# GpSimd makes three of the sixteen u*B products of a state-space scan

## The chip, the cores and the metric

The kernel runs on one core of one Trainium2 chip. The metric is the device time of one launch in microseconds. Before the change it is 1684.95 us, the median of three runs (1680.35 to 1686.84).

## The reference

A decoder block in float32 on x of shape (4, 1024, 256): a state-space block (Mamba), cross attention over 154 context positions with 16 heads, and a mixture of four experts with the best two weighted, each with a residual and a layer norm. The change touches the first.

```python
x_ssm, z = split(x @ W_in.T)                 # 512 channels each
x_ssm = silu(causal_conv(x_ssm, 4 taps) + conv_b)
proj = x_ssm @ W_x.T                         # B (16), C (16), dt (1) per token
dt = softplus(proj[..., -1:] * W_dt + b_dt)
A = -exp(A_log)                              # (512, 16)
def step(h, inp):                            # over 1024 tokens
    dA = exp(dt_t[..., None] * A)
    h = dA * h + (x_t * dt_t)[..., None] * B_t[:, None, :]
    y = einsum('bdn,bn->bd', h, C_t)
y = (y + x_ssm * D) * silu(z)
x = layernorm(x + y @ W_out.T)
```

## The kernel before

The tokens are worked in 16 chunks of 256 (four per batch). Channels lie on the partitions: 512 channels are four tiles, so u, dt, a decay or a state of one state index n is 128 x 4 x 256. A chunk runs through n = 0 to 15, each in two halves h of two channel tiles (128x512).

For each n, TensorE spreads B's row over the partitions in PSUM (`b_row`, L368); VectorE multiplies it with u into one of three PSUM banks (`make_bu`, L945), adds the carried state to the first column where the chunk isn't a batch's first (`add_carry`, L961) and scans: state = decay * previous + u*B (`scans`, L970). ScalarE makes the decays, exp(dt*A), four instructions for an n (`step`, L686), and copies the last column of a state out (L684). GpSimd multiplies the state by C (L900), and TensorE transposes and adds these into y (`add_state`, L384). Decay, state and state*C each have a ring of four buffers. In the first column of each tile the decay is zero, so that the two tiles of a half don't mix.

While chunk i is scanned, chunk k = i + 1 is prepared and chunks i - 1 and i - 2 are finished. Nothing schedules this at run time: each engine has a list of (place, work), and work with place n stands behind its instructions for state n of chunk i. On TensorE, at each place, `b_row(n + 2)` and `add_state(n - 2)` stand ahead of the work. The places that matter here:

- TensorE: input projection 0 and 1, convolution halves 2 and 4 (`conv`, L305), z tiles 5 and 6 (L316), `project` 8.
- ScalarE: `take_xi` 3 and 4, `take_conv` 5 and 7 (L595), `take_z` 8 and 9 (L600), silus 10, `copies` 11 (L616, L617), `terms` and `softplus` 12 (L632 to L642), `next_lead` 13 (L626), `take_y_back` 14 and 15. The norm of chunk i - 2: `spreads` 3, `guess` 6, `normalise` 9 (L667).
- GpSimd: `split` 8 and 10 (L844, L848), `make_dt` 10 (L814, waits for the softplus), `first_arg` 10, `make_u` 11 (L819), `injections` 12 and 4 (L836); the norm: `centre` 0 (L863), `variance` 2, `newton` 4 (L868 to L878), on tiles of two columns.
- VectorE: `take_y` of chunk i - 1 (L933) inside state 2.

SyncE stores each chunk's C rows to DRAM and loads them back spread over all partitions (`load_c`). In the first chunk it also loads all weights of the attention and the experts. The second block (`attn_ffn_block`) starts when the first has ended.

## Time and profile before

| what | value |
|---|---|
| median of three runs | 1684.95 us |
| the profiled execution | 1675.18 us, span 1673.4 us |
| VectorE busy | 1465.3 us (88%) |
| TensorE busy (matmuls) | 1335.8 us (80%) |
| ScalarE busy | 1114.0 us (67%) |
| GpSimd busy | 915.1 us (55%) |
| mean granted TensorE clock | 0.919 |
| state-space block | about 0 to 999 us |

Busy time is the time in which at least one instruction runs on the engine. Successive instructions of VectorE, ScalarE and GpSimd overlap by some hundredths of a microsecond, so what one costs in a full queue is read from start to start. In the trace "step_area" is dt and u (and later the rows of maxima), "c_area" the spread C rows, "weights" the convolution's input and weights, "y_sb" also the z tile.

### The profile page before, as it was taken

To read this page: it belongs to the slowest core of one execution; us is meant where nothing else is said; L and a number is where in the kernel's file an instruction comes from. 1 tells how busy PE (TensorE), PEld (TensorE's weight loads), DVE (VectorE), ACT (ScalarE), POOL (GpSimd) and SP (SyncE) were. 2 spreads that over 40 slices of the span, in tenths; PEclk is the share of its full clock that TensorE was granted. 3 is DMA by queue.
4 is the path that set the end of the run, shared out by engine and by line. 5 is a ranking of instruction groups with operands and counts; after the bars stand their busy time and mean duration, and the time that the engine had idled before them with its cause. 6 is when DMAs were issued, how large, how long until landed. Compare 5 with 4: busy or idle time off the path is not lost. (4 is left out here: it accounts for less than half of the span.)

```text
span 1673.4 us, 22601 instructions
## 1 busy us (share of the span) xinstructions
PE 1335.8 (80%) x7484; PEld 930.7 (56%) x7484; DVE 1465.3 (88%) x2698; ACT 1114.0 (67%) x2452; POOL 915.1 (55%) x663
## 2 busy tenths in 40 slices
PE   7687778788777877787886969988988898887880
PEld 5566556666656666565665644446445644462460
DVE  5999999999999999999999966697869786978578
ACT  5867887788788778878877524337633763375570
POOL 1778878877887788788778701102710271027015
PEclk9889899989989898998898989999999999999895
DMA  7201210220122022102102012100010000000000
GB/s 234 67 14 45 70 58 13 70 70 32 40 70 71 1 70 70 50 21 70 64 1 89 14 38 103 36 1 1 26 55 1 1 26 26 1 1 1 25 1 25
DMA packets 37927, 69.87 MB, mean 42 GB/s; under 512 B 3569, under 2 KB 31570, under 8 KB 33586
## 3 DMA queue, kind: packets, MB, share of 16 engines
q1 hardware_dynamic: 37810, 68.43, 12.0%
q8 instruction: 59, 0.97, 0.2%
q14 instruction: 58, 0.48, 0.1%
HBM read 59.77 MB, written 8.65 MB: 41 GB/s over the span
## 5 line engine op out<-in xcount | busy, mean ns | idle before, releaser
L900 POOL TENSOR_TENSOR state_c<-state,c_area 128x1024 f32<-128x1024 f32 x256 | 602.0, 2362 | 167.8 <-DVE state L970 148.9
L970 DVE TENSOR_TENSOR_SCAN state<-decay,ps 128x512 f32<-128x512 f32 x512 | 620.6, 1212 | 0.0
L686 ACT ACTIVATE decay<-step_area,negA 128x255 f32<-128x255 f32 x1024 | 432.6, 496 | 0.4 <-DVE step_area L1049 0.4
L945 DVE TENSOR_TENSOR ps<-step_area,ps 128x512 f32<-128x512 f32 x512 | 349.7, 683 | 8.0 <-PE ps L368 6.2
L384 PE MATMUL ps<-ident_sb,state_c 128*128 128x128 f32 x2048 | 293.3, 291 | 12.9 <-POOL state_c L900 11.9
L1578 POOL TENSOR_TENSOR big<-big,g_sb 128x1024 f32<-128x1024 f32 x29 | 79.4, 2739 | 406.6 <-ACT big L1467 404.9
L384 PEld LDWEIGHTS ps<-ident_sb,state_c 128*128 128x128 f32 x2048 | 253.5, 151 | 39.0 <-POOL state_c L900 21.5
L368 PE MATMUL ps<-parts,sel_bc_sb 96*128 96x256 bf16 x256 | 74.7, 292 | 102.7 <-DVE ps L961 80.2
L1391 PE MATMUL ps<-w_sb,weights 128*128 128x512 f32 x256 | 122.6, 615 | 0.0
L1426 PE MATMUL ps<-w_sb,hT 128*128 128x256 f32 x512 | 120.0, 388 | 2.4 <-ACT hT L1536 1.9
L1666 DVE BATCH_NORM_STATS2 stats<-big 128x6 f32<-128x256 f32 x256 | 88.4, 413 | 30.4 <-ACT big L1541 21.1
L368 PEld LDWEIGHTS ps<-parts,sel_bc_sb 96*128 96x128 bf16 x256 | 25.8, 101 | 151.3 <-DVE ps L961 113.5
L305 PE MATMUL ps<-weights 128*128 128x256 f32 x480 | 108.5, 378 | 0.0
L1426 PEld LDWEIGHTS ps<-w_sb,hT 128*128 128x128 f32 x512 | 96.8, 194 | 18.7 <-ACT hT L1536 5.1
L1646 DVE TENSOR_REDUCE step_area<-ps 128x8 f32<-128x1232 f32 x48 | 69.0, 1437 | 34.0 <-PE ps L1287 33.9
L1521 ACT ACTIVATE big<-ps 128x1024 f32<-128x1024 f32 x32 | 32.8, 1024 | 98.3 <-PE ps L1391 98.3
L305 PEld LDWEIGHTS ps<-weights 128*128 128x128 f32 x480 | 88.5, 189 | 11.2
L1582 POOL TENSOR_TENSOR acc<-acc,big 128x256 f32<-128x256 f32 x116 | 86.3, 744 | 9.1
L288 PE MATMUL ps<-weights 128*128 128x256 f32 x240 | 64.0, 414 | 29.7 <-ACT weights L586 29.7
L356 PE MATMUL ps<-w_out_sb,y_sb 128*128 128x256 f32 x256 | 77.2, 456 | 0.0
L1478 ACT ACTIVATE hT<-ps 128x1024 f32<-128x1024 f32 x64 | 62.0, 1020 | 20.1 <-PE ps L1319 20.1
L1391 PEld LDWEIGHTS ps<-w_sb,weights 128*128 128x128 f32 x256 | 45.8, 192 | 49.6 <-issue 47.3
(211 smaller groups left out, 2357.9 us busy)
## 6 DMA issues: line engine op xcount, KB each, us to landing
c_area<-c_scratch SPq DMA_DIRECT2D x32, 1024.0 KB, 6.5
weights<-in_xT SPq DMA_DIRECT2D x16, 256.0 KB, 3.1
...
weights<-x_scratch SPq DMA_DIRECT2D x4, 1024.0 KB, 8.1
xa<-x_scratch SPq DMA_DIRECT2D x4, 1024.0 KB, 5.6
out_x<-acc SPq DMA_DIRECT2D x4, 1024.0 KB, 4.4
w_sb<-in_w SPq DMA_DIRECT2D x2, 1024.0 KB, 13.0
```

Source lines behind the costliest of these rows:

```text
L305: last = nc.tensor.matmul(w_ps[:, e * TC + skip:(e + 1) * TC], diag_w[:, TAPS - 1 - back, j, :], xi[:, j, HALO + skip - back:HALO + TC - b ...
L368: nc.tensor.matmul(b_ps[n % 2][:, 0:TC], sel_bc_sb[:, n, :], parts[:, i[1] % 2, :], start=True, stop=True)\
L384: last = nc.tensor.matmul(y_ps[:, t * DI + j * P:t * DI + (j + 1) * P], state_c[:, n % RING, j, t * P:(t + 1) * P], ident_sb[:, :], start= ...
L686: nc.scalar.activation(decay[:, n % RING, j, 1:], dt_sb[:, i[1] % 2, j, 1:], ACT.Exp, scale=negA[:, j * NS + n:j * NS + n + 1]).then_inc(s ...
L900: nc.gpsimd.tensor_tensor(state_c[:, n % RING, :, :], state[:, n % RING, :, :], c_bc[:, q, n, :].unsqueeze(1).to_broadcast([P, CT, TC]), A ...
L945: nc.vector.tensor_tensor(bu_ps[m % 3][:, :].rearrange("p (j n) -> p j n", j=2), u_sb[:, i[1] % 2, 2 * h:2 * h + 2, :], b_ps[n % 2][:, 0:T ...
L970: nc.vector.tensor_tensor_scan(state[:, n % RING, pair, :].rearrange("p j n -> p (j n)"), decay[:, n % RING, pair, :].rearrange("p j n -> ...
L1391: last = nc.tensor.matmul(dst, xT[:, k, t * P:(t + 1) * P], w1_sb[:, k, h * HALF:(h + 1) * HALF], start=False, stop=k == KT - 1, skip_grou ...
L1426: last = nc.tensor.matmul(dst, hT[:, e * KT + k, i * P:(i + 1) * P], w2_sb[:, e * KT + k, :], start=False, stop=k == KT - 1, skip_group_ch ...
L1578: nc.gpsimd.tensor_tensor(tile, tile, g2_sb[:, :], ALU.mult).then_inc(s_gm, 1)
L1582: nc.gpsimd.tensor_tensor(acc[:, t, :], acc[:, t, :], tile[:, e * DM:(e + 1) * DM], ALU.add).then_inc(s_sum, 1)
L1666: nc.vector.bn_stats(stats[:, i * E + e, :], big[:, n, i, e * DM:(e + 1) * DM]).then_inc(s_st, 1)
```

## The change

For n = 2, 5 and 8 (`OFF`) GpSimd multiplies u by B's row into a new SBUF tile `ub` (two buffers) and adds the carried state there. The B rows for this come through DRAM like the C rows, into `b_bc`. The PSUM bank that had held u*B of these n now takes their decay: ScalarE writes zeros into its first columns and the exponentials into the rest, one step later than the decays of the other n, and waits for the bank (`psum_decay`). The scan of these n reads decay from PSUM and u*B from SBUF. TensorE leaves out their B rows.

GpSimd's norm uses operations with two constants in place of pairs, and its places and ScalarE's change. The loads of w1 and w2 move to the start of the second block, since their space is taken.

```diff
+        OFF, APART = (2, 5, 8), 3
+        KEPT = [n for n in range(NS) if n not in OFF]
...
             def load_c(k):
-                sp.dma_start(c_dram[bass.ds(at(k, NS), NS), :], proj[NS:BC, q, :]).then_inc(s_cst, 16)
+                sp.dma_start(bc_dram[bass.ds(at(k, BC), BC), :], proj[0:BC, q, :]).then_inc(s_cst, 16)
...
+                if not is_first(k):
+                    sp.wait_ge(s_ub, at(k, 2 * NO))
+                rows = bc_dram[bass.ds(at(k, BC, OFF[0]), APART * NO), :].rearrange("(a s) n -> a s n", s=APART)
+                sp.dma_start(b_bc[:, :, :], rows[:, 0, :].partition_broadcast(P)).then_inc(s_bb, 16)
...
             def step(i, n):
...
+                if n in KEPT:
+                    for j in range(CT):
+                        nc.scalar.activation(decay_tile(i, n)[:, j, 1:], dt_sb[:, i[1] % 2, j, 1:], ACT.Exp,
+                                             scale=negA[:, j * NS + n:j * NS + n + 1]).then_inc(s_decay, 1)
+                if n - 1 in OFF:
+                    psum_decay(i, n - 1)
+
+            def psum_decay(i, n):
+                for h in range(2):
+                    act.wait_ge(s_scan, bu_free(i, n, h))
+                    bank = bu_bank(i, n, h)[:, :].rearrange("p (j n) -> p j n", j=2)
+                    nc.scalar.activation(bank[:, :, 0], zeros[:, :], ACT.Copy)
+                    for e in range(2):
+                        j = 2 * h + e
+                        nc.scalar.activation(bank[:, e, 1:], dt_sb[:, i[1] % 2, j, 1:], ACT.Exp,
+                                             scale=negA[:, j * NS + n:j * NS + n + 1]).then_inc(s_decay, 1)
...
-                    work += [... (3, lambda: spreads(old)), (6, lambda: guess(old)),
-                             (9, lambda: normalise(old))]
+                    work += [... (5, lambda: spreads(old)), (8, lambda: guess(old)),
+                             (13, lambda: normalise(old))]
...
+            def product_b(i, n):
+                c, later = OFF.index(n), i[1] % CPB
...
+                nc.gpsimd.tensor_tensor(tile, u_sb[:, i[1] % 2, :, :], b_bc[:, c, :].unsqueeze(1).to_broadcast([P, CT, TC]),
+                                        ALU.mult).then_inc(s_ub, 1 if later else 2)
+                if later:
...
+                    pool.wait_ge(s_ub, at(i, 2 * NO, 2 * c + 1))
+                    nc.gpsimd.tensor_tensor(tile[:, :, 0], tile[:, :, 0], inject[:, n, :], ALU.add).then_inc(s_ub, 1)
...
-                    work += [(0, lambda: centre(old)), (2, lambda: variance(old)), (4, lambda: newton(old))]
+                    work += [(0, lambda: centre(old)), (3, lambda: variance(old)), (6, lambda: newton(old))]
...
+                work += [(1, lambda: product_b(i, OFF[1])), (4, lambda: product_b(i, OFF[2]))]
+                if prepare:
+                    work.append((14, lambda: product_b(k, OFF[0])))
...
             def scans(i, n, h):
...
+                if n in OFF:
...
+                    a, b = bu_bank(i, n, h)[:, :], flat(ub_tile(i, n))
+                else:
...
+                    a, b = flat(decay_tile(i, n)), bu_bank(i, n, h)[:, :]
...
-        LOADS = 4
+        LOADS = 6
+            sp.dma_start(w1_sb[:, :, :], w1).then_inc(s_const, 16)
+            sp.dma_start(w2_sb[:, :, :], w2).then_inc(s_const, 16)
```

GpSimd before, from `make_dt` (step_area<-step_area,relu) to the norm's variance of the next chunk; step_area<-step_area,xs is `make_u`:

```order
L814 TENSOR_TENSOR step_area<-step_area,relu 128x1024 [waits s_sp]
L826 TENSOR_TENSOR first_dA<-step_area,negA 128x64 [waits s_dt]
L848 TENSOR_TENSOR parts<-rest,lead 96x256 [waits s_lead]
L900 TENSOR_TENSOR state_c<-state,c_area 128x1024 [waits s_sum,s_scan]
L819 TENSOR_TENSOR step_area<-step_area,xs 128x1024 [waits s_dt]
L900 TENSOR_TENSOR state_c<-state,c_area 128x1024 [waits s_sum,s_scan]
L836 TENSOR_TENSOR inject<-first_dA,carry 128x48 [waits s_carry,s_dA]
L900 TENSOR_TENSOR state_c<-state,c_area 128x1024 [waits s_sum,s_scan] x3
L900 TENSOR_TENSOR state_c<-state,c_area 128x1024 [waits s_sum,s_scan,s_cb10]
L863 TENSOR_TENSOR mean<-total,coef 128x2 [waits s_r,s_norm]
L900 TENSOR_TENSOR state_c<-state,c_area 128x1024 [waits s_sum,s_scan] x2
```

The same place now, from the injections on:

```order
L891 TENSOR_TENSOR inject<-first_dA,carry 128x48 [waits s_carry,s_dA]
L972 TENSOR_TENSOR state_c<-state,c_area 128x1024 [waits s_sum,s_scan] x2
L941 TENSOR_TENSOR ub<-step_area,b_bc 128x1024 [waits s_scan,s_bb,s_u]
L947 TENSOR_TENSOR ub<-ub,inject 128x4 [waits s_ub,s_inj]
L972 TENSOR_TENSOR state_c<-state,c_area 128x1024 [waits s_sum,s_scan]
L972 TENSOR_TENSOR state_c<-state,c_area 128x1024 [waits s_sum,s_scan,s_cb10]
L915 TENSOR_SCALAR mean<-total 128x2 [waits s_r,s_norm]
L972 TENSOR_TENSOR state_c<-state,c_area 128x1024 [waits s_sum,s_scan]
L941 TENSOR_TENSOR ub<-step_area,b_bc 128x1024 [waits s_scan]
L947 TENSOR_TENSOR ub<-ub,inject 128x4 [waits s_ub]
L972 TENSOR_TENSOR state_c<-state,c_area 128x1024 [waits s_sum,s_scan] x2
```

One product with its small add stands between state*C 14 and 15, and one between state*C 1 and 2.

ScalarE before, from the second convolution half (xs<-ps,par_sb) to the silus, places 7 to 10; y_sb<-ps is a z tile:

```order
L595 ACTIVATE xs<-ps,par_sb 128x256 [waits s_in]
L595 ACTIVATE xs<-ps,par_sb 128x256
L684 ACTIVATE carry<-state 128x4 [waits s_scan]
L686 ACTIVATE decay<-step_area,negA 128x255 x4
L600 ACTIVATE y_sb<-ps 128x512 [waits s_in]
L684 ACTIVATE carry<-state 128x4 [waits s_scan]
L686 ACTIVATE decay<-step_area,negA 128x255 x4
L667 ACTIVATE res<-res,shift_sb,rstd 128x256 [waits s_nw]
L667 ACTIVATE res<-res,shift_sb,rstd 128x256
L600 ACTIVATE y_sb<-ps 128x512 [waits s_in]
```

The same place now:

```order
L637 ACTIVATE xs<-ps,par_sb 128x256 [waits s_in]
L637 ACTIVATE xs<-ps,par_sb 128x256
L724 ACTIVATE carry<-state 128x4 [waits s_scan]
L715 ACTIVATE lnv<-var 128x2 [waits s_nw]
L717 ACTIVATE rstd<-lnv 128x2 [waits s_ln]
L642 ACTIVATE y_sb<-ps 128x512 [waits s_in]
L724 ACTIVATE carry<-state 128x4 [waits s_scan]
L728 ACTIVATE decay<-step_area,negA 128x255 x4
L738 ACTIVATE ps<-zeros 128x2 [waits s_scan]
L741 ACTIVATE ps<-step_area,negA 128x255 x2
L738 ACTIVATE ps<-zeros 128x2 [waits s_scan]
L741 ACTIVATE ps<-step_area,negA 128x255 x2
```

Between the convolution and z tile 0 there is no decay any more; behind z tile 0 stand decay 9 and then decay 8, in PSUM. The normalisation has left this place.

VectorE now, from the carry add of state 0's second half to state 3 (order prints a scan as SCALAR_TENSOR_TENSOR; yg is `take_y`):

```order
L1033 TENSOR_TENSOR ps<-ps,inject 128x2 [waits s_bu]
L1017 TENSOR_TENSOR ps<-step_area,ps 128x512 [waits s_scan]
L1049 SCALAR_TENSOR_TENSOR state<-decay,ps 128x512 [waits s_decay,s_bu,s_sc]
L1033 TENSOR_TENSOR ps<-ps,inject 128x2 [waits s_bu]
L1049 SCALAR_TENSOR_TENSOR state<-decay,ps 128x512 [waits s_decay,s_bu]
L1049 SCALAR_TENSOR_TENSOR state<-ps,ub 128x512 [waits s_decay,s_ub,s_sc]
L1003 TENSOR_TENSOR yg<-ps,gate 128x1024 [waits s_gate,s_yb,s_sum]
L1017 TENSOR_TENSOR ps<-step_area,ps 128x512 [waits s_scan,s_b]
L1049 SCALAR_TENSOR_TENSOR state<-ps,ub 128x512 [waits s_decay]
```

Before, a product and a carry add stood ahead of each scan; now two products with their carry adds are missing here.

## Rows read from the trace of the kernel before

**Rows 1.** Windows: busy us of each engine (instructions), granted clock, DMA share, GB/s.
```profile
300.00:360.00 60.00, 46.89 (x264) 36.73 (x262) 59.76 (x92) 48.61 (x125) 46.97 (x33) 0.91 0.17 58
```

**Rows 2.** The page's part 5, the costliest groups of the block.
```profile
L900 POOL TENSOR_TENSOR state_c<-state,c_area 128x1024 f32<-128x1024 f32 x256 | 602.0, 2362 | 167.8 <-DVE state L970 148.9
L970 DVE TENSOR_TENSOR_SCAN state<-decay,ps 128x512 f32<-128x512 f32 x512 | 620.6, 1212 | 0.0
...
L945 DVE TENSOR_TENSOR ps<-step_area,ps 128x512 f32<-128x512 f32 x512 | 349.7, 683 | 8.0 <-PE ps L368 6.2
```

**Rows 3.** Timeline (start us, duration us, instruction), VectorE's `take_y`, four chunks apart.
```profile
268.51 1.20 DVE L933 TENSOR_TENSOR yg<-ps,gate 128x1024 f32<-128x1024 f32 x1
...
500.58 1.20 DVE L933 TENSOR_TENSOR yg<-ps,gate 128x1024 f32<-128x1024 f32 x1
```

**Rows 4.** Timeline of VectorE, half a state.
```profile
401.33 0.15 DVE L961 TENSOR_TENSOR ps<-ps,inject 128x2 f32<-128x2 f32 x1
401.38 0.68 DVE L945 TENSOR_TENSOR ps<-step_area,ps 128x512 f32<-128x512 f32 x1
401.98 1.21 DVE L970 TENSOR_TENSOR_SCAN state<-decay,ps 128x512 f32<-128x512 f32 x1
403.11 0.15 DVE L961 TENSOR_TENSOR ps<-ps,inject 128x2 f32<-128x2 f32 x1
```

**Rows 5.** Timeline of GpSimd, from `make_dt` to the next chunk's `centre`.
```profile
420.30 2.36 POOL L814 TENSOR_TENSOR step_area<-step_area,relu 128x1024 f32<-128x1024 f32 x1 [2.18 <-ACT step_area L642]
...
423.10 0.67 POOL L848 TENSOR_TENSOR parts<-rest,lead 96x256 bf16<-96x256 f32 x1
...
430.90 9.33 POOL L900 TENSOR_TENSOR state_c<-state,c_area 128x1024 f32<-128x1024 f32 x4
440.19 0.19 POOL L863 TENSOR_TENSOR mean<-total,coef 128x2 f32<-128x2 f32 x1
```

**Rows 6.** Timeline of TensorE, `add_state(2)` and the second convolution half.
```profile
392.78 1.04 PE L384 MATMUL ps<-ident_sb,state_c 128*128 128x128 f32 x8
393.66 3.62 PE L305 MATMUL ps<-weights 128*128 128x256 f32 x16
```

**Rows 7.** Timeline of ScalarE, from the second convolution half to `next_lead`.
```profile
397.32 0.84 ACT L595 ACTIVATE xs<-ps,par_sb 128x256 f32<-128x256 f32 x2 [2.39 <-PE ps L305]
...
398.14 1.70 ACT L686 ACTIVATE decay<-step_area,negA 128x255 f32<-128x255 f32 x4
400.23 0.60 ACT L600 ACTIVATE y_sb<-ps 128x512 f32<-128x512 f32 x1 [0.39 <-PE ps L316]
...
402.42 1.08 ACT L667 ACTIVATE res<-res,shift_sb,rstd 128x256 f32<-128x256 f32 x2
...
421.82 0.49 ACT L626 ACTIVATE lead<-rest,par_sb 96x256 bf16<-96x256 f32 x1
```

**Rows 8.** Timeline of GpSimd, two dependent small operations of the norm.
```profile
396.99 0.20 POOL L870 TENSOR_TENSOR newt<-newt,var 128x2 f32<-128x2 f32 x1
397.26 0.20 POOL L872 TENSOR_TENSOR newt<-newt,coef 128x2 f32<-128x2 f32 x1
```

**Rows 9.** Line 1578, later block: durations ns min/median/max, first and last start us.
```profile
L1578 POOL TENSOR_TENSOR big<-big,g_sb x29: 2354/2366/4667, 1158.7 to 1649.0; 128x1024 f32<-128x1024 f32 x29
```

**Rows 10.** Line 814, `make_dt`, in the same form.
```profile
L814 POOL TENSOR_TENSOR step_area<-step_area,relu x15: 2349/2358/2365, 72.7 to 884.5; 128x1024 f32<-128x1024 f32 x15
```

**Rows 11.** The page's part 6, loads of w1 and w2.
```profile
w_sb<-in_w SPq DMA_DIRECT2D x2, 1024.0 KB, 13.0
```

**Rows 12.** The last constant's issue; VectorE's first wait behind the constants (line 1775).
```profile
1002.01 0.43 SPq L1201 DMA_DIRECT2D before_sb<-in_before  x1
...
L1775 DVEq EVENT_SEMAPHORE  x4: 21/21/50, 1035.8 to 1533.4; - x4
```

**Rows 13.** Timeline of TensorE behind an idle time of 2.39 us.
```profile
406.87 0.40 PE L368 MATMUL ps<-parts,sel_bc_sb 96*128 96x256 bf16 x1 [2.39 <-DVE ps L961]
407.05 1.92 PE L384 MATMUL ps<-ident_sb,state_c 128*128 128x128 f32 x8
```

More of the change, by code:

```diff
@@ L43, with mamba_block @@
 TG = 4
-def mamba_block(nc, x, xT, w_in, w_x, w_out, par, ident_sb, ident, sel_bc, sel_p, c_dram, x1, ahead, s_ahead, ps, early, late, shared,
+def mamba_block(nc, x, xT, w_in, w_x, w_out, par, ident_sb, ident, sel_bc, sel_p, bc_dram, x1, ahead, s_ahead, ps, early, late, shared,
                 w, ctxT):
@@ L64, in mamba_block @@
         SKIP_AT = 8
+        OFF, APART = (2, 5, 8), 3
+        KEPT = [n for n in range(NS) if n not in OFF]
+        NO, NK = len(OFF), len(KEPT)
+        USERS = [(n, h) for n in range(NS) for h in range(2)]
+        EMIT = []
+        for n in range(NS):
+            if n in KEPT:
+                EMIT.append(n)
+            if n - 1 in OFF:
+                EMIT.append(n - 1)
         w_ssm, diag_w, xi, w_gate, xT_sb, w_x_sb = (early[n] for n in ("w_ssm", "diag_w", "xi", "w_gate", "xT", "w_x"))
@@ L83, in mamba_block @@
         state_c = sb("state_c", [P, RING, CT, TC])
+        ub = sb("ub", [P, 2, CT, TC])
+        b_bc = sb("b_bc", [P, NO, TC])
+        zeros = sb("zeros", [P, 2])
         carry = sb("carry", [P, NS, CT])
@@ L130, in mamba_block @@
         s_par = sem("s_par")
-        s_coef = sem("s_coef")
         s_in = sem("s_in")
@@ L148, in mamba_block @@
         s_bu = sem("s_bu")
+        s_ub = sem("s_ub")
+        s_bb = sem("s_bb")
         s_scan = sem("s_scan")
@@ L186, in shift, with rank, scanned, bu_bank @@
             return (i[0], i[1] + n)
+        def rank(n):
+            return sum(m < n for m in KEPT)
+        def scanned(i, n, h):
+            return at(i, 2 * NS, 2 * RING + 2 * n + h + 1)
+        def bu_bank(i, n, h):
+            return bu_ps[at(i, len(USERS), USERS.index((n, h))) % 3]
+        def bu_free(i, n, h):
+            p = USERS.index((n, h))
+            return scanned(i if p >= 3 else shift(i, -1), *USERS[p - 3])
+        def decay_tile(i, n):
+            return decay[:, at(i, NK, rank(n)) % RING, :, :]
+        def ub_tile(i, n):
+            return ub[:, at(i, NO, OFF.index(n)) % 2, :, :]
         def is_first(i):
@@ L364, in b_row @@
             def b_row(i, n):
+                if n in OFF:
+                    return
                 if n == 0:
                     pe.wait_ge(s_split, at(i, 2, 2))
-                pe.wait_ge(s_bu, at(i, 4 * NS, 4 * n + 4))
+                before = n - 4 if n - 2 in OFF else n - 2
+                if before >= 0:
+                    pe.wait_ge(s_bu, at(i, 4 * NK, 8 + 4 * rank(before) + 4))
+                else:
+                    pe.wait_ge(s_bu, at(i, 4 * NK, 4 * n + 4))
                 nc.tensor.matmul(b_ps[n % 2][:, 0:TC], sel_bc_sb[:, n, :], parts[:, i[1] % 2, :], start=True, stop=True)\
@@ L905, in turn @@
                             what()
+            nc.gpsimd.memset(zeros[:, :], 0.0)
             nc.gpsimd.memset(decay[:, :, :, 0], 0.0).then_inc(s_zero, 1)
-            for c, value in enumerate((0.5, 1.5, 1.0 / DM, LN_EPS, -1.0 / DM)):
-                nc.gpsimd.memset(coef[:, c, :], value).then_inc(s_coef, 1)
-            half, one_half, per_dm, eps, minus_per_dm = (coef[:, c, :] for c in range(5))
             pool.sem_inc(s_sum, RING)
@@ L917, in _ @@
             injections(first, 0, NS - RING)
+            product_b(first, OFF[0])
             turns(pool, turn)
@@ L1063, in _, with attn_ffn_block @@
             round_neg(1)
-def attn_ffn_block(nc, x1, ctxT, ident_sb, w, ps, late, shared, bo, g2, be2, bias_rows, before, out):
+def attn_ffn_block(nc, x1, ctxT, ident_sb, w, w1, w2, ps, late, shared, bo, g2, be2, bias_rows, before, out):
     U = G * NL
@@ L1931, in decoder_block @@
             ahead.append((w[name][tuple(slice(None) for _ in shape)], source))
-        mamba_block(nc, x, xT, w_in, w_x, w_out, par, ident_sb, ident, sel_bc, sel_p, c_dram, x1, ahead, s_ahead, ps, early, late,
+        mamba_block(nc, x, xT, w_in, w_x, w_out, par, ident_sb, ident, sel_bc, sel_p, bc_dram, x1, ahead, s_ahead, ps, early, late,
                     shared, w, ctxT)
-        attn_ffn_block(nc, x1, ctxT, ident_sb, w, ps, late, shared, bo, g2, be2, bias_rows, before, out)
+        attn_ffn_block(nc, x1, ctxT, ident_sb, w, channels(w1), channels(w2), ps, late, shared, bo, g2, be2, bias_rows, before, out)
 def _constants():
```

96 lines of the change are left out of this document (52 added, 44 removed).

## Prediction

> **What bounds the kernel now.** I read the page first. Part 1 has VectorE busy for 88% of the span; the slices of part 2 show that in the first 58% (the state-space block) it is full, while ScalarE and GpSimd are at seven or eight tenths. A 60 us window in the middle has VectorE at 59.76 of 60, ScalarE at 48.61 and GpSimd at 46.97 [rows 1]. The costly groups are the scans, the u*B products and GpSimd's state*C [rows 2]. So each chunk lasts as long as VectorE needs. Two of VectorE's `take_y`, four chunks apart, are at 268.51 and 500.58 [rows 3]: 58.0 us a chunk.
>
> Durations on VectorE overlap, so I take start to start from its timeline [rows 4]: carry add 0.05, product 0.60, scan 1.13, together 1.78 for half a state, 3.55 for a state. 16 x 3.55 plus 1.1 for `take_y` is 57.9; a batch's first chunk has no carry adds.
>
> Then I looked for the second longest thing: a ring of waits through three engines that closes once a chunk. I call D the start of GpSimd's `make_dt` (L814). From D GpSimd runs without a gap to its `centre`, 420.30 to 440.19, 19.9 us [rows 5]; this covers the make_dt and make_u of the next chunk and the state*C of states 11 to 15 and 0. Then come state*C 1 and 2. TensorE's `add_state(2)` needs state*C 2, and the second convolution half stands behind it in TensorE's order: 0.88 from add to convolution [rows 6], 3.66 to ScalarE's `take_conv(k, 1)` at 397.32 [rows 6, 7]. From there ScalarE works to the softplus, which releases the next D: 23.0 us, 397.32 to 420.30 [rows 5, 7]. The sum is 19.9 + 0.2 (centre) + 2.33 + 2.36 (state*C, a quarter of the 9.33 of four, and a last one in full) + 0.05 + 0.88 + 3.66 + 23.0 = 52.4 us. It is under 57.9, so today this ring has 5.5 us of slack and VectorE rules.
>
> **VectorE.** For states 2, 5 and 8 two products and two carry adds go: 6 x (0.60 + 0.05) = 3.9 us a chunk, 3.6 in a batch's first chunk. Against it, `add_carry(n-1, 1)` now stands directly ahead of its scan, without a product between: 0.1 us each, three times (the carry add is 0.15 long and 0.05 of that is hidden now [rows 4]). The scans keep their shape and one operand in PSUM, so 1.13 stays. Net 3.6 a chunk: VectorE alone would need 54.3.
>
> **GpSimd.** A product is a 128x1024 two-input operation, as state*C with 2.36 [rows 2, 5]. The carry add behind it waits for it: a waiting small operation starts 0.07 after the one before and takes 0.20 [rows 8]. So 2.6 us, three times a chunk: 7.8. The norm loses two small operations, 2 x 0.27 [rows 8]. GpSimd's busy 46.97 of 60 is 45.4 of 58.0; it becomes some 52.7. By itself that is still under 54.3. But two of the three products (state 2 at place 14, state 5 at place 1) lie inside the ring's GpSimd part: +5.2. What waits behind the one at place 1 is state*C 2, and for that TensorE with its convolution. The product of state 8 (place 4) lies outside the ring.
>
> The rule that could make this product dearer is the Trainium skill's "GPSIMD Engine Reference", section 1: GpSimd's SBUF interface is shared with VectorE, with contention when VectorE has two SBUF inputs. The same form on GpSimd in the later block has a median of 2366 ns and a maximum of 4667 [rows 9], which that could be. The new scan reads decay from PSUM and u*B from SBUF, one SBUF input as before, so by that rule too 2.36 holds; with 4.67 for each product the ring would be 4.6 us longer.
>
> **ScalarE.** The decays of 2, 5 and 8 are written one step later, behind those of 3, 6 and 9, and each half waits for its PSUM bank. What counts is the ring's part. Before, decay 8 (1.70, at 398.14) lay in the time in which ScalarE waited for TensorE's z tile at 400.23 [rows 7]: it cost nothing. Now only `guess` stands there, and decay 8 follows decay 9, behind z tile 0, on the path: +1.6, and two writes of zeros, for which no row stands: between the 0.05 of a hidden small operation [rows 4] and the 0.27 of a waiting one [rows 8] I take 0.1 each: +1.8. The norm's `normalise` (1.08, of which 0.1 overlaps) leaves the stretch: -0.98. It now stands ahead of `next_lead`, which was at 421.82 with 0.49 [rows 7], so the lead is ready at 423.3 where GpSimd's `parts` started at 423.10 [rows 5]: +0.25. The exponentials that write PSUM have no row. Bounds: the SBUF form is 0.42 each (1.70 for four), the one that reads PSUM is 0.42 (0.84 for two) [rows 7]; I take 0.40 start to start, bounds 0.2 and 0.6, which moves the ring by 0.8 us either way. The Trainium skill ("ScalarE: Activation LUTs", Profile) says that PSUM is the lower-latency destination for ScalarE; no row here shows it, and it would speak for the lower half.
>
> **The ring afterwards.** 52.4 + 5.2 + 1.8 - 0.98 + 0.25 = 58.6 us (57.9 where the chunk is a batch's first: an injection and two small adds are missing, each 0.2 to 0.27 as in [rows 8]). That is more than VectorE's 54.3 and a little more than today's 58.0. So VectorE gets a wait of about 4 us a chunk, and the chunk is not shorter.
>
> Other ways round are shorter. Via convolution half 0, decay 6, the late decay 5, and the rest of ScalarE to the softplus: 22.7 (GpSimd to the end of state*C 0) + 5.2 + 0.8 + 1.8 + 1.9 + 1.8 + 23.8 = 58.0, close behind. Via VectorE's scan 7, which frees the bank of decay 8's second half: about 57.
>
> **The sum.** L814 runs from 72.7 (chunk 1) to 884.5 (chunk 15) [rows 10]: 14 turns in 811.8 us. Now 3 x 57.9 + 11 x 58.6 = 818.3: +6.5. The first D comes about 1 us later (decay 8's 1.8 less some 0.8 that VectorE is ahead by then). The last chunk prepares no next one, so the ring is open there and VectorE's gain counts: up to -3.9; ScalarE's transposes of the attention stand in that chunk, so -3 (bounds -3.9 and 0). Together +4.5.
>
> The rest is hidden. w1 and w2 (1 MB each; two such took 13.0 us to land [rows 11]) are issued after 1002.01, and the first wait of VectorE behind the constants passes at 1035.8 [rows 12]: 33 us of cover; without it, up to 10 us. Their absence at the start frees queue time that nobody waited for. The small store of B and C and the load of three rows of B are asked for at ScalarE's copies and needed at place 14, over 10 us later. The shorter norm in the tail stands beside VectorE's row of maxima: 0.
>
> On the profiled execution's time: 1675.2 + 4.5 = 1679.7. That execution is 9.8 below the median of 1684.95; against the median, which is what I forecast for, 1684.95 + 4.5 = 1689.
>
> **Rivals.** B: VectorE stays the bound, because the ring has an overlap that I count in series. Full busy share in [rows 1] speaks for it, the sum above against. Then 12 x 3.6 + 4 x 3.4 = 57 us less: 1628.
>
> C, the slower side: TensorE's clock. Today TensorE's b_row waits for VectorE in small pieces; in the new order it waits for state*C 2 after an early convolution half 0, some 1.4 to 2 us idle, just ahead of the second half. After 2.39 us idle at 406.87, eight transposes took 1.92, against 1.04 at 392.78 [rows 6, 13]: the 1.2 GHz level against 2.4. At that level add_state is 0.9 longer and the convolution's 3.46 doubles. It decides if TensorE idles there as long as it did at 406.87. If the clock falls in every chunk, that is +4.3 x 14 = 60 us: 1749; in half of them, 1719. For it: the ring leaves TensorE longer idle. Against: in the rows the slow stretch followed on other sparse time, and the convolution stands behind a busy stretch.
>
> E: the ring is shorter than I sum it, mostly by cheaper PSUM writes and small overlaps, near 57.5 a chunk: -15 in 14 turns, and -3 in the last: 1668.
>
> **How the numbers follow.** The measurement can tell about 0.5% (8.4 us) from no change. Forecast 0.50; of it 0.42 within 0.5% (bounds of the PSUM writes and the last chunk: -5 to +8), 0.08 slower, where the rings next to it interfere. B 0.15, faster. C 0.27, slower. E 0.08, faster. So faster 0.23, same 0.42, slower 0.35. Range: from 1660, which takes in E but not B, to 1730, which takes in C in two chunks of three; left out are B and the last third of C, about 0.2.
>
> **What would show it.** Right: L814 about 58.5 apart, VectorE at some 93% of a chunk, its waits on ScalarE's or GpSimd's result, GpSimd without a gap from make_dt to state*C 2, ScalarE's decay 8 behind z tile 0. Wrong: VectorE still at 99% with D 54 to 55 apart (B); convolution groups of 6 us with the granted clock at 0.5 (C); products on GpSimd well over 2.4 us.

## The result, and the profile after

The changed kernel takes 1692.74 us (median; 1689.78 to 1695.24, without one execution of 2077.16 us in which the granted clock was 0.61), beside 1681.24 us of the kernel before on the same chip (1676.16 to 1686.84, seven runs). The ratio is 1.0065, 95% interval 1.0042 to 1.0088: slower, by little. 1689 was forecast, from a median of before that was 1684.95 then. The forecast difference was +4.5 us; the medians differ by 11.5. The two profiled executions differ by 17.6 (1692.74 and 1675.18), because the profiled execution of before is 6 us under its median.

The first look is at GpSimd's `make_dt`, now L869, in the form of [rows 10] (durations in ns, first and last start in us):

```profile
L869 POOL TENSOR_TENSOR step_area<-step_area,relu x15: 2347/2350/2363, 76.8 to 897.1; 128x1024 f32<-128x1024 f32 x15
```

Fourteen turns take 897.1 - 76.8 = 820.3 us, 58.6 each; before they took 58.0. The same window as in [rows 1], then a long one of both kernels, after first (busy us of TensorE's matmuls, its weight loads, VectorE, ScalarE and GpSimd, with instructions; granted clock, DMA share, GB/s):

```profile
300.00:360.00 60.00, 45.43 (x257) 36.48 (x256) 54.82 (x76) 48.95 (x132) 52.77 (x36) 0.90 0.15 56
100.00:900.00 800.00, 616.12 (x3426) 498.26 (x3423) 743.79 (x1084) 649.41 (x1721) 714.54 (x471) 0.90 0.16 57
```

```profile
100.00:900.00 800.00, 629.91 (x3507) 504.82 (x3505) 794.97 (x1243) 649.66 (x1668) 629.92 (x430) 0.91 0.15 52
```

VectorE, which was busy for 99% of the block, now idles 56 of 800 us, 4.1 a chunk. Its busy time fell from 57.6 to 54.5 us a chunk, and all of it came back as idle time. What it waits for, of the kernel after, grouped by line between 100 and 900 us (busy us and mean ns, then idle us ahead of the group and who ended it; L1049 are scans, L1017 u*B products, L1003 `take_y`):

```profile
L1049 DVE TENSOR_TENSOR_SCAN state<-decay,ps 128x512 f32<-128x512 f32 x355 | 429.1, 1211 | 3.3 <-ACT decay L728 2.0
L1017 DVE TENSOR_TENSOR ps<-step_area,ps 128x512 f32<-128x512 f32 x356 | 243.2, 683 | 33.6 <-issue 17.4 <-PE ps L410 16.1
L1049 DVE TENSOR_TENSOR_SCAN state<-ps,ub 128x512 f32<-128x512 f32 x83 | 100.6, 1213 | 6.9 <-ACT ps L741 6.1
L1003 DVE TENSOR_TENSOR yg<-ps,gate 128x1024 f32<-128x1024 f32 x13 | 15.9, 1224 | 12.4 <-issue 12.4
```

One turn in detail. GpSimd from one `make_dt` to state*C 2, to compare with [rows 5] (start, duration, instruction, idle time before it in brackets; ub is the new product):

```profile
427.50 2.35 POOL L869 TENSOR_TENSOR step_area<-step_area,relu 128x1024 f32<-128x1024 f32 x1 [2.25 <-ACT step_area L684]
...
430.57 0.67 POOL L903 TENSOR_TENSOR parts<-rest,lead 96x256 bf16<-96x256 f32 x1 [0.23 <-ACT lead L668]
...
443.02 2.37 POOL L941 TENSOR_TENSOR ub<-step_area,b_bc 128x1024 f32<-128x1024 f32 x1
445.54 0.20 POOL L947 TENSOR_TENSOR ub<-ub,inject 128x4 f32<-128x4 f32 x1
445.69 4.66 POOL L972 TENSOR_TENSOR state_c<-state,c_area 128x1024 f32<-128x1024 f32 x2
...
452.81 2.36 POOL L941 TENSOR_TENSOR ub<-step_area,b_bc 128x1024 f32<-128x1024 f32 x1
455.25 0.20 POOL L947 TENSOR_TENSOR ub<-ub,inject 128x4 f32<-128x4 f32 x1
455.39 2.36 POOL L972 TENSOR_TENSOR state_c<-state,c_area 128x1024 f32<-128x1024 f32 x1
```

TensorE behind it, as [rows 6]:

```profile
458.35 0.28 PE L410 MATMUL ps<-parts,sel_bc_sb 96*128 96x256 bf16 x1 [0.47 <-DVE ps L1033]
458.47 1.04 PE L426 MATMUL ps<-ident_sb,state_c 128*128 128x128 f32 x8
459.35 3.60 PE L341 MATMUL ps<-weights 128*128 128x256 f32 x16
```

ScalarE behind that, as [rows 7], from `take_conv(k, 1)` to the second z tile:

```profile
462.99 0.84 ACT L637 ACTIVATE xs<-ps,par_sb 128x256 f32<-128x256 f32 x2
...
465.90 0.60 ACT L642 ACTIVATE y_sb<-ps 128x512 f32<-128x512 f32 x1 [1.65 <-PE ps L352]
466.39 0.20 ACT L724 ACTIVATE carry<-state 128x4 f32<-128x4 f32 x1
466.49 1.69 ACT L728 ACTIVATE decay<-step_area,negA 128x255 f32<-128x255 f32 x4
468.08 0.15 ACT L738 ACTIVATE ps<-zeros 128x2 f32<-128x2 f32 x1
468.18 0.86 ACT L741 ACTIVATE ps<-step_area,negA 128x255 f32<-128x255 f32 x2
468.97 0.15 ACT L738 ACTIVATE ps<-zeros 128x2 f32<-128x2 f32 x1
469.07 0.86 ACT L741 ACTIVATE ps<-step_area,negA 128x255 f32<-128x255 f32 x2
469.86 0.58 ACT L642 ACTIVATE y_sb<-ps 128x512 f32<-128x512 f32 x1
```

This is the predicted ring: GpSimd has no gap but the 0.23 on the lead, state*C 2 ends 30.2 us after D, the convolution follows, and decay 8 stands behind z tile 0, 1.78 us from its first zero to the next z tile. The next D comes at 486.77, 23.8 us after `take_conv`. One row differs: `b_row(6)`, ahead of `add_state(2)` in TensorE's order, waited for VectorE until 458.35, some 0.6 after GpSimd's result was there. A branch through VectorE runs beside the ring and was last in this turn. ScalarE came to `take_conv` without idle time, where [rows 7] have 2.39: the decays ahead of it, the late one of 5 among them, had just ended.

This turn is one of three of 59.2 to 59.3 us. The three in which a batch's first chunk is scanned took 57.8 to 57.9, the other eight 58.4 to 58.75. What the three long ones have in common is the second half of TensorE's input projection: 2.93, 3.32 and 2.88 us, where the other eleven took 1.89. The granted clock was 0.64, 0.55 and 0.65 in these stretches and 1.00 at 390.26. The projection of the turn shown, then that of the turn before it (D at 368.75), with what follows there on TensorE and, last, ScalarE's `take_conv(k, 1)`:

```profile
449.65 2.93 PE L324 MATMUL ps<-weights 128*128 128x256 f32 x8
```

```profile
390.26 1.89 PE L324 MATMUL ps<-weights 128*128 128x256 f32 x8
...
398.92 0.28 PE L410 MATMUL ps<-parts,sel_bc_sb 96*128 96x256 bf16 x1 [1.45 <-DVE ps L1033]
399.06 1.09 PE L426 MATMUL ps<-ident_sb,state_c 128*128 128x128 f32 x8
399.99 3.62 PE L341 MATMUL ps<-weights 128*128 128x256 f32 x16
...
403.65 0.84 ACT L637 ACTIVATE xs<-ps,par_sb 128x256 f32<-128x256 f32 x2 [1.02 <-PE ps L341]
```

In this ordinary turn state*C 2 ends at 399.0, 30.3 after D, `take_conv` comes 4.6 later and the next D 23.85 after that: 58.75. `b_row(6)` was only 0.1 ahead of `add_state(2)`, so the branch through VectorE is about as long here too.

Where the 17.6 us of the two profiled executions are:

| stretch | before | after | difference |
|---|---|---|---|
| start to the first D | 72.7 | 76.8 | +4.1 |
| 14 turns | 811.8 | 820.3 | +8.5 |
| last D to the last scan | 72.6 | 76.4 | +3.8 |
| rest | 716.3 | 717.5 | +1.2 |

### The profile page after: what moved, and what is told of

Read it like the earlier page. It is cut to its first block and busy times, and to the rows that moved or that the text cites. A ratio compares the mean times of both kernels' runs of the same rounds, so it can differ in the third digit from the quotient of the medians.

```text
span 1691.0 us, 22427 instructions
## 1 busy us (share of the span) xinstructions
PE 1333.7 (79%) x7436; PEld 934.6 (55%) x7436; DVE 1412.8 (84%) x2530; ACT 1123.9 (66%) x2548; POOL 1023.6 (61%) x711
## 5 line engine op out<-in xcount | busy, mean ns | idle before, releaser
L1049 DVE TENSOR_TENSOR_SCAN state<-decay,ps 128x512 f32<-128x512 f32 x416 | 502.6, 1211 | 4.3 <-ACT decay L728 2.8
L728 ACT ACTIVATE decay<-step_area,negA 128x255 f32<-128x255 f32 x832 | 351.4, 496 | 0.5 <-DVE step_area L1127 0.5
L426 PE MATMUL ps<-ident_sb,state_c 128*128 128x128 f32 x2048 | 296.2, 293 | 53.5 <-POOL state_c L972 53.2
L1017 DVE TENSOR_TENSOR ps<-step_area,ps 128x512 f32<-128x512 f32 x416 | 284.0, 683 | 45.3 <-PE ps L410 26.1
L426 PEld LDWEIGHTS ps<-ident_sb,state_c 128*128 128x128 f32 x2048 | 256.2, 152 | 97.3 <-POOL state_c L972 72.7
L941 POOL TENSOR_TENSOR ub<-step_area,b_bc 128x1024 f32<-128x1024 f32 x48 | 113.4, 2362 | 28.7 <-DVE step_area L1130 28.7
L1049 DVE TENSOR_TENSOR_SCAN state<-ps,ub 128x512 f32<-128x512 f32 x96 | 116.4, 1212 | 10.5 <-ACT ps L741 9.2
L341 PE MATMUL ps<-weights 128*128 128x256 f32 x480 | 108.5, 378 | 0.0
L383 PE MATMUL ps<-ident_sb,yg 128*128 128x128 f32 x128 | 26.9, 347 | 82.6 <-ACT y_sb L688 70.2
L361 PE MATMUL ps<-xs,weights 128*97 128x256 f32 x120 | 49.6, 585 | 44.3 <-ACT xs L648 44.3
L410 PE MATMUL ps<-parts,sel_bc_sb 96*128 96x256 bf16 x208 | 61.9, 298 | 27.4 <-DVE ps L1033 20.9
L741 ACT ACTIVATE ps<-step_area,negA 128x255 f32<-128x255 f32 x192 | 82.3, 460 | 0.0
```

Source lines behind the costliest of these rows:

```text
L341: last = nc.tensor.matmul(w_ps[:, e * TC + skip:(e + 1) * TC], diag_w[:, TAPS - 1 - back, j, :], xi[:, j, HALO + skip - back:HALO + TC - b ...
L426: last = nc.tensor.matmul(y_ps[:, t * DI + j * P:t * DI + (j + 1) * P], state_c[:, n % RING, j, t * P:(t + 1) * P], ident_sb[:, :], start= ...
L728: nc.scalar.activation(decay_tile(i, n)[:, j, 1:], dt_sb[:, i[1] % 2, j, 1:], ACT.Exp, scale=negA[:, j * NS + n:j * NS + n + 1]).then_inc( ...
L941: nc.gpsimd.tensor_tensor(tile, u_sb[:, i[1] % 2, :, :], b_bc[:, c, :].unsqueeze(1).to_broadcast([P, CT, TC]), ALU.mult).then_inc(s_ub, 1 ...
L1017: nc.vector.tensor_tensor(bu_bank(i, n, h)[:, :].rearrange("p (j n) -> p j n", j=2), u_sb[:, i[1] % 2, 2 * h:2 * h + 2, :], b_ps[n % 2][:, ...
L1049: nc.vector.tensor_tensor_scan(state[:, n % RING, pair, :].rearrange("p j n -> p (j n)"), a, b, 0.0, ALU.mult, ALU.add).then_inc(s_scan, 1)
```

## Experiments

All ratios are to the kernel before, run on the same chip in turns. "D to D" is the start of `make_dt` in the last chunk less that in the first, over 14, and VectorE's idle time is that between 100 and 900 us.

| kernel | ratio (95% interval) | D to D | VectorE idle |
|---|---|---|---|
| before | 1 | 58.0 | 5.0 |
| after | 1.0065 (1.0042 to 1.0088) | 58.6 | 56.2 |
| before, gate cut | 1.0008 (0.9980 to 1.0036) | 58.2 | 7.8 |
| after, gate cut | 1.0005 (0.9980 to 1.0030) | 57.95 | 49.3 |
| before, extra products | 1.0200 (1.0165 to 1.0236) | 60.2 | 2.3 |
| after, extra products | 1.0103 (1.0065 to 1.0141) | 58.6 | 26.2 |
| after, state 5's product at place 2 | 1.0044 (1.0017 to 1.0072) | 58.3 | 53.2 |
| before with the norm's part alone | 0.9980 (0.9949 to 1.0010) | 58.0 | 6.1 |
| states 8, 11, 14 | 1.0136 (1.0099 to 1.0173) | 59.6 | 71.8 |
| states 6, 9 | 1.0069 (1.0041 to 1.0096) | 58.5 | 45.7 |
| states 3, 6, 9 | 1.0030 (1.0008 to 1.0053) | 57.9 | 54.6 |
| states 2, 5 | 0.9968 (0.9943 to 0.9992) | 57.4 | 28.2 |
| states 2, 5; 5 at place 2 | 0.9964 (0.9947 to 0.9980) | 57.3 | 27.7 |
| state 2 | 0.9889 (0.9864 to 0.9914) | 57.1 | 11.0 |

### Who bounds each kernel

Two pairs test it from both sides. The first makes ScalarE's part of the ring shorter, in both kernels: the gate's silu, one instruction of 1.0 us, works on 16 of its 1024 columns from the third chunk on.

```diff
-                nc.scalar.activation(gate[:, q, :, :], zc[:, :, :], ACT.Silu).then_inc(s_gate, 1)
+                few = DI if k[1] < 2 else 8
+                nc.scalar.activation(gate[:, q, :, 0:few], zc[:, :, 0:few], ACT.Silu).then_inc(s_gate, 1)
```

> The kernel before, with ScalarE's silu of the gate cut to 16 of its 1024 columns from chunk 2 on (the output is then not the reference's). It stands in ScalarE's stretch between the second convolution half and the softplus and takes 1.04 us there. Ring theory (before, the ring ScalarE - GpSimd - TensorE has 5.5 us of slack and VectorE rules): no change, 1681, within 0.2%. Rival (ScalarE's work bounds the chunk in both kernels): 13 x 0.95 = 12 us less, 1669.

> The changed kernel with the same cut of the gate's silu (output not the reference's). Ring theory (the ring closes and bounds the chunk): make_dt to make_dt gets 0.95 shorter, 13 x 0.95 = 12 us less than the changed kernel's 1692.7, so 1680, about level with before. Rival 1 (VectorE still bounds, and what it gained is lost in waits for the late decays in PSUM): under 4 us. Rival 2 (GpSimd's 52.7 us of work bound it): 0.

The kernel before took 1681.39 us, no change. The one after took 1684.18, 8.5 under its 1692.74; its turn fell from 58.6 to 57.95. So a microsecond of ScalarE's time is worth nothing before and most of a microsecond a chunk after. That less than the whole came back (0.65 a turn) has two parts in the trace: the turns with a batch's first chunk hardly moved (57.85 to 57.8), and the ordinary ones fell by 0.8 (58.6 to 57.8). A second way round close behind would do that; which one was not settled.

The second pair makes VectorE's work longer: four products more in a chunk, into a spare tile.

```diff
+                if n in (10, 12):
+                    dve.wait_ge(s_extra, at(i, 4, (n - 10) + h))
+                    nc.vector.tensor_tensor(spare[:, :, :], ...).then_inc(s_extra, 1)
```

> The kernel before with VectorE making four more products of 128x512 per chunk (n = 10 and 12, into a spare tile that nobody reads): 4 x 0.6 = 2.4 us of VectorE per chunk. Ring theory (VectorE rules before): 16 x 2.4 = 38 us more, 1719. Rival (VectorE was not the bound before): under 10 us.

> The changed kernel with the same four extra products of VectorE per chunk. Ring theory: VectorE has some 4 us of waits in each chunk, so most of the 2.4 is hidden; 0 to 10 us more than 1692.7, so 1693 to 1703, and most of it in the last chunk (2.4) and where VectorE's delay meets TensorE's b_row. Rival 1 (VectorE bounds): 38 us more, 1731.

Before: 1710.96 us, 2.0% slower, and a turn of 60.2, +2.2 for 2.4 us of work. That is some 5 us less in all than expected. Some of it is idle time that VectorE still had and has no more (5.0 to 2.3 us in 800, 0.2 a turn); the rest stays unexplained. After: 1695.36 (ratio 1.0103 beside 1.0065, with intervals that overlap), and the turn is 58.6 as without them; VectorE's idle time fell from 56.2 to 26.2 us. `make_dt` of the kernel before with the extra products, then of after with them:

```profile
L816 POOL TENSOR_TENSOR step_area<-step_area,relu x15: 2347/2355/2365, 71.8 to 914.7; 128x1024 f32<-128x1024 f32 x15
```

```profile
L871 POOL TENSOR_TENSOR step_area<-step_area,relu x15: 2352/2358/2367, 75.7 to 896.1; 128x1024 f32<-128x1024 f32 x15
```

Before, VectorE is the bound; after, it has room for 2.4 us of work more. Both pairs together show the exchange of the bound, and exclude rival B.

### The parts of the change

The product of state 5 one place later, so that it stands behind state*C 2 and not ahead of it:

```diff
-                work += [(1, lambda: product_b(i, OFF[1])), (4, lambda: product_b(i, OFF[2]))]
+                work += [(2, lambda: product_b(i, OFF[1])), (4, lambda: product_b(i, OFF[2]))]
```

> The changed kernel with one number changed: GpSimd's product of state 5 at place 2 instead of 1, so behind state*C 2, on which TensorE's add_state(2) and the second convolution half wait. Ring theory, GpSimd branch (state*C 2 releases the second convolution half): 2.6 us leave the ring, but the next ring (VectorE's take_y and b_row(6), or the first half with decays 6 and 5) is only 0.6 shorter, so 0.3 to 0.8 us a chunk, 4 to 11 us less: 1682 to 1689. If the trace's branch through take_y and b_row(6) rules (there the second half started 0.6 us after add_state(2) could have): 0 to 3 us less. Rival (GpSimd's amount of work bounds): 0.

The time, 1690.07, is 2.7 us less, as the branch through VectorE would have it (0 to 3). A turn fell by 0.27 us on average, not by 2.6. The three turns with a batch's first chunk fell from 57.85 to 57.0; the ordinary ones stayed at 58.3 to 58.7. In those a way round that does not lead through state*C 2 is as long as the ring, and takes over at once. `b_row(6)` above is the likely one, and `take_y` another (it waited 1.04 us in the turn shown).

The norm's part alone, on the kernel before (fewer operations, their places, ScalarE's places):

> The kernel before with only the norm's part of the change: GpSimd's two operations fewer and the later places of the norm on GpSimd and ScalarE. Ring theory (VectorE rules before, the norm stands beside it): no change from before, within 0.2%. Rival (the norm's chain costs the chunk time): 2 to 5 us less.

1678.84 us, ratio 0.9980 with an interval that holds 1; first and last D at 72.7 and 884.5, as in [rows 10] to the digit. It does nothing where VectorE is the bound.

States 2 and 5 alone, state 8 as before (`OFF, APART = (2, 5), 3`, no product at place 4):

> The changed kernel with states 2 and 5 alone (state 8 as before: VectorE's product, decay in SBUF, made ahead of z tile 0). Ring theory: decay 8 leaves the path, 1.8 us less a chunk, 58.6 to 56.8; VectorE alone needs 57.9 - 2.4 = 55.5. So 14 x 1.8 = 25 us less than the changed kernel, with 2 to 5 lost again to rings beside it: 1668 to 1674, which is faster than before although VectorE keeps one product more. Rival (every product moved saves or costs the same): the change's +11 in proportion, 2/3 of it, 1689.

1675.95 us, ratio 0.9968, a turn of 57.4 instead of 58.6. That is short of the 1668 to 1674 that I expected: state 8 cost 1.2 us a chunk, of the 1.8 that its late decay is long on the path; its product lay outside. Two states moved is faster than three. Against before there is little in it: the last scan starts at 957.2 us in this trace and at 957.1 in that of before.

### Other choices of the states

If what stands in the ring decides, then states should be chosen by where their products and late decays fall. The first try had all three products outside GpSimd's part, at places 4, 6 and 9:

```diff
-        OFF, APART = (2, 5, 8), 3
+        OFF, APART = (8, 11, 14), 3
...
-                work += [(1, lambda: product_b(i, OFF[1])), (4, lambda: product_b(i, OFF[2]))]
-                if prepare:
-                    work.append((14, lambda: product_b(k, OFF[0])))
+                work += [(4, lambda: product_b(i, OFF[0])), (6, lambda: product_b(i, OFF[1])), (9, lambda: product_b(i, OFF[2]))]
...
```

> The changed kernel with states 8, 11 and 14 in place of 2, 5 and 8, and GpSimd's products at places 4, 6 and 9 of the same chunk: the same work, all three products outside the ring's GpSimd part (make_dt to state*C 2). Ring theory: the ring is 58.6 - 5.2 + 0.2 = 53.6; VectorE alone needs 54.3, GpSimd alone 53.9. So 54.5 to 56 us a chunk, 2 to 3.5 less than before's 58.0: 28 to 49 less than before in 14 turns, and a last chunk that is not longer; 1640 to 1660. Rival (the amount of GpSimd's work, or the form with decay in PSUM, bounds it): no change from the changed kernel, 1685 to 1693.

All of it missed: 1702.86 us, the slowest of the states tried. VectorE's scans of the moved states wait for their decays, 51.5 us between 100 and 900. Those scans grouped, then one of them (state 14), behind decays 13 and 15, `take_y_back` and the norm's `normalise`, all of which ScalarE has to do between softplus and the late decay of 14:

```profile
L1048 DVE TENSOR_TENSOR_SCAN state<-ps,ub 128x512 f32<-128x512 f32 x80 | 97.1, 1213 | 51.5 <-ACT ps L741 51.5
...
437.07 1.22 DVE L1048 TENSOR_TENSOR_SCAN state<-ps,ub 128x512 f32<-128x512 f32 x1 [2.76 <-ACT ps L741]
```

A late decay can be written only when the bank is free, and the third half-state scan after that one needs it, where an ordinary decay has a ring of four buffers. A VectorE held up here frees `b_row(6)` late, and with it TensorE's convolution behind. That is another ring, through VectorE, that my sum did not have; it is read from these rows, and no run took it apart.

The second and third try put late decays at places where ScalarE has little to do, with the products outside GpSimd's part (6, 9 at places 3 and 5; 3, 6, 9 with 3 at place 14):

```diff
-        OFF, APART = (2, 5, 8), 3
+        OFF, APART = (6, 9), 3
...
```

> The changed kernel with states 6 and 9 in place of 2, 5, 8, their products at places 3 and 5 of the same chunk on GpSimd. Decay 6 in PSUM then stands where ScalarE waited for the second convolution half anyway, decay 9 behind decay 10 in the stretch (+0.2 to 0.6), and no product lies between make_dt and state*C 2. Three rings: ScalarE-GpSimd-TensorE 52.5; VectorE alone 55.3; the ring that closed in the kernel with states 8, 11, 14 (softplus, decay 13, VectorE's states 13 to 4, b_row(6), second convolution half, ScalarE) 1.1 + 27.2 + 4.7 + 22.6 = 55.6. So 55.6 to 56.2 a chunk, 14 x 2 = 25 to 34 us less than before: 1650 to 1660. Rival (the form with decay in PSUM costs as much as it saves): 1682.

> The changed kernel with states 3, 6, 9 and the products at places 14 (state 3, in the chunk before), 3 and 5. One product (2.6) lies in the ring ScalarE-GpSimd-TensorE: 52.5 + 2.6 = 55.1. VectorE alone 54.3; the ring through VectorE's states 13 to 4 is shortened by state 3's 1.3: 54.3. So 55.1 to 56 a chunk, 14 x 2 to 2.9 = 28 to 41 us less than before: 1642 to 1656. Rival: as the changed kernel, 1690.

Both missed too: 1691.96 and 1685.17 us. The trace of states 6 and 9 shows what the expectation left out. ScalarE's order around the late decay of 6, which stands ahead of `take_conv(k, 1)`:

```profile
397.38 0.17 ACT L738 ACTIVATE ps<-zeros 128x2 f32<-128x2 f32 x1 [1.59 <-DVE state L1048]
397.49 0.85 ACT L741 ACTIVATE ps<-step_area,negA 128x255 f32<-128x255 f32 x2
399.15 0.18 ACT L738 ACTIVATE ps<-zeros 128x2 f32<-128x2 f32 x1 [0.81 <-DVE state L1048]
399.26 0.86 ACT L741 ACTIVATE ps<-step_area,negA 128x255 f32<-128x255 f32 x2
400.06 0.82 ACT L637 ACTIVATE xs<-ps,par_sb 128x256 f32<-128x256 f32 x2
```

The late decay waits until VectorE has scanned the bank's last user, 1.59 and 0.81 us here, 31.1 us between 100 and 900 in all. The PSUM ring has three banks of half a state, so at a late decay ScalarE can't be more than a state and a half ahead of VectorE. Everything behind that wait, the path to the softplus included, starts later.

The last two runs went back to states 2 and 5, and to state 2 alone (only place 14 is left of the three):

```diff
-        OFF, APART = (2, 5, 8), 3
+        OFF, APART = (2,), 3
...
-                work += [(1, lambda: product_b(i, OFF[1])), (4, lambda: product_b(i, OFF[2]))]
```

> The changed kernel with OFF = (2,): only state 2's product on GpSimd (place 14), so GpSimd's part of the ring holds one product instead of two and ScalarE's part no late decay. Ring theory: the ring is 52.4 + 2.6 - 1.0 + 0.25 = 54.3 us (with the 0.5 by which the other sums fell short, 54.8), VectorE alone needs 57.9 - 1.3 + 0.1 = 56.7. VectorE is the longer one: a chunk is 56.7 to 57.0, shorter than with states 2 and 5 (57.4) although VectorE does MORE work. The time is 0.990 to 0.995 of before's, under the 0.9968 of states 2 and 5. Rival, the number of products decides (each moved product saves VectorE time): above that of states 2 and 5, 0.998. Rival, the late decay of state 2 and its wait hold ScalarE back: no change against before, first make_dt 3 to 4 us later as in the changed kernel.

> States 2 and 5 on GpSimd, with the product of state 5 at place 2 instead of 1, that is behind state*C 2, for which TensorE's second convolution half waits. Ring theory: this product (2.6 us) leaves the ring through state*C 2, which falls to some 54.8; VectorE alone needs 57.9 - 2.6 + 0.2 = 55.5, and the branches beside the ring (take_y behind add_state(15), b_row(6)) gave back only 0.27 in the same move with three states. So a chunk of 56 to 57.2 instead of 57.4, the time 0.987 to 0.995 of before's. Rival, the ring at 57.4 runs by a way in which state*C 2 doesn't stand: no change against states 2 and 5 at place 1, 0.9968.

State 2 alone takes 1665.38 us, ratio 0.9889 (0.9864 to 0.9914), a little faster than expected and the fastest of all: 1.1% under before, and by the two ratios 1.7% under after. Its turn is 57.1 us, a little over the 56.7 to 57.0 expected. VectorE is the bound again, busy for 789 of 800 us. Its idle time, in the kernel with state 2 alone:

```profile
L1048 DVE TENSOR_TENSOR_SCAN state<-decay,ps 128x512 f32<-128x512 f32 x420 | 508.9, 1212 | 0.4
L1016 DVE TENSOR_TENSOR ps<-step_area,ps 128x512 f32<-128x512 f32 x419 | 286.2, 683 | 1.1 <-PE ps L410 0.8 <-issue 0.3
...
L1002 DVE TENSOR_TENSOR yg<-ps,gate 128x1024 f32<-128x1024 f32 x14 | 17.1, 1225 | 9.5 <-issue 9.4
```

and its `make_dt`:

```profile
L869 POOL TENSOR_TENSOR step_area<-step_area,relu x15: 2347/2358/2362, 74.7 to 874.4; 128x1024 f32<-128x1024 f32 x15
```

The 9.5 us ahead of `take_y` (0.7 a chunk) are most of what is left.

Not all of the 1.1% need be the product. The last scan starts at 946.1 us in this trace and at 957.1 in that of before: 11.0 us, 0.65%, where the medians differ by 18.7. The kernel before took 1672 to 1689 us in its 17 executions beside this one, at mean granted clocks of 0.923 down to 0.909, the longer ones mostly at the lower clock; the six with state 2 alone had 0.914 to 0.925. Where the clock can cost that much is seen in the last chunk, of the kernel before with the gate cut and then of the kernel before (values' projection of the attention, granted clock 0.50 and 1.00):

```profile
919.43 3.75 PE L437 MATMUL ps<-wv_sb,ctx_sb 128*128 128x512 f32 x4 [0.88 <-ACT weights L694]
```

```profile
917.12 1.95 PE L437 MATMUL ps<-wv_sb,ctx_sb 128*128 128x512 f32 x4 [1.52 <-ACT weights L693]
```

From the last D to the last scan the first took 81.0 us and the second 72.6, with nothing moved to GpSimd in either; the gate cut only takes work from ScalarE. That the clock makes this difference is read from these rows, and no run took it apart.

With states 2 and 5 the place of the second product made no difference (1678.79 us, 0.9964 beside 0.9968), so my expectation missed and its rival held: at 57.3 the way round does not lead through state*C 2. Only the turns with a batch's first chunk fell clearly, from 56.6 to 55.7. Which way it takes was not settled. The trace has VectorE waiting for ScalarE's late decay of 5 (1.14 us ahead of that scan in one chunk) and for `take_y` (0.83 in the same one).

## Why the prediction was right

**The mechanism and its size.** A ring of 58.6 us a chunk was forecast (57.9 with a batch's first chunk), and the turns took 58.6 on average, in place of VectorE's 58.0. The pairs of gate and extra products show that VectorE bound before and not after. VectorE alone was put at 54.3 and its wait at about 4: it was busy for 54.5 and idled 4.1 a chunk. The size came out larger than forecast. +4.5 us was forecast, the medians differ by 11.5; and 0.65% is over the 0.5% that I called telling, so it is "slower, where the rings next to it interfere", which I gave 0.08, and not the "within 0.5%" that had 0.42.

**The terms of GpSimd and ScalarE.** The 48 products took 2.345 to 2.397 us, nothing near 4.67, beside a VectorE that scans with one operand in SBUF. D to the end of state*C 2 is 457.75 - 427.50 = 30.25 us, as the terms 19.9 + 0.2 + 2.33 + 2.36 + 5.2 and 0.25 for the lead give. The late decay of 8 took 1.78 for 1.8 forecast, and `take_conv` to D 23.8 for 23.0 + 1.8 - 0.98. What I had to bound between 0.2 and 0.6, the exponential into PSUM, is 0.40 from start to start, as taken (0.89 from zero to zero with two of them and the zero's 0.10). That other ways round are close behind was right as well, though I had them at 58.0 and 57: taking 2.6 or 1.0 us out of the ring gave back 0.27 and 0.65.

**Where the ring's exact sum holds, and where it is luck.** Between state*C 2 and `take_conv` I took 0.05 + 0.88 + 3.66 = 4.6. The ordinary turn from 368.75 has 4.6, and the eight such turns took 58.6 on average; the three with a batch's first chunk took 57.8 to 57.9 for 57.9. In the turn shown first it was 462.99 - 457.75 = 5.2. But when state 5's product left the ring, the ordinary turns stayed at 58.6. So a second way round, through VectorE or the first convolution half, is as long as the one that I summed, and not the 58.0 that I had for the longest of the others. That the two agree so closely is luck.

**The mis-sized terms.** The 14 turns were forecast at +6.5 and gave +8.5, 820.3 us for 818.3. All of the 2.0 is in the three long turns, 0.7 each. Their second input projection ran at a granted clock of 0.55 to 0.65; in one of them (683.55) it began no later after D than in an ordinary turn, so there the clock fell before the turn was late. The trace of after with the extra products has three turns of 59.2 to 59.5, and in them and no other the second projection took 2.7 to 3.3 us.

The first D was forecast at +1 and gave +4.1. In the first chunk VectorE is not ahead, ScalarE waits at the late decay of 2 for its bank (0.50 and 0.74 us), and the input's copy behind it is 1.9 us late. TensorE idles for it, and the projection that follows runs at the lower of its clocks (granted 0.50; before 1.00). The kernel with state 2 alone has the same waits and the same slow projection, and its first D is at 74.7, 2.0 later than before; with states 2 and 5 it is at 75.7. With states 8, 11 and 14, where no late decay stands there, the projection took 1.99. The 76.8 is itself at the high end: three more traces with states 2, 5 and 8 have 75.3 to 75.7. TensorE in the first chunk after, then the same projection before:

```profile
37.47 3.78 PE L324 MATMUL ps<-weights 128*128 128x256 f32 x8 [2.60 <-ACT weights L628]
```

```profile
35.55 1.99 PE L288 MATMUL ps<-weights 128*128 128x256 f32 x8 [0.72 <-ACT weights L586]
```

The last chunk was forecast at -3 and gave +3.8, the largest miss. I reasoned that without a next chunk the ring is open and VectorE's gain counts. But the late decays with their waits stand in that chunk too, ahead of ScalarE's copies for the attention, and TensorE's rows of B stand behind those. ScalarE's wait at the late decay of 5, of after, and then VectorE's for TensorE:

```profile
925.42 0.17 ACT L738 ACTIVATE ps<-zeros 128x2 f32<-128x2 f32 x1 [1.75 <-DVE state L1049]
...
927.19 0.17 ACT L738 ACTIVATE ps<-zeros 128x2 f32<-128x2 f32 x1 [0.81 <-DVE state L1049]
...
936.44 0.70 DVE L1017 TENSOR_TENSOR ps<-step_area,ps 128x512 f32<-128x512 f32 x1 [6.84 <-PE ps L410]
```

The chain is read from these rows; no run took it apart. From the last D to the last scan it is 72.6 us before, 72.0 with the norm's part alone and 71.7 with state 2 alone, and 76.4 in after and with state 5's product at place 2; in all five the values' projection ran at the full clock. So the +3.8 repeats. But this stretch alone reached 81.0 where that projection ran at the lower clock, in the kernel before with the gate cut, so one trace of it says little. All three misses, 3.1 + 2.0 + 6.8 us, go the same way. In the first and the last chunk I priced the late decay by its length and gave its wait for the bank nothing; in the turns I gave TensorE's clock nothing in the forecast itself.

**The rivals.** B (VectorE stays the bound, 1628) is excluded by the two pairs. C (TensorE's clock falls ahead of the second convolution half) did not occur: all 480 convolution matmuls took 374 to 382 ns, before and after alike, and the mean granted clock is 0.912 beside 0.919. The clock did fall elsewhere, in the input projection, at the start and in three of the 14 turns, for 0.7 us a turn and not 4.3. E (a shorter ring) did not occur. Its 1668 was a slip as well: 57.5 a chunk is 14 x 57.5 = 805 for 811.8, 7 us less and not 15, so E stands for some 1676.

**Hidden loads.** The rest differs by 1.2 us. It is 718.2 and 720.3 us in two traces with w1 and w2 loaded as before (gate cut, norm's part alone) and 713.1 to 720.4 in those with the loads moved, so no cost of the move shows, as forecast.
